# Both halves of every odd mixture chunk on GpSimd, VectorE casting the even chunks only

## What is computed

```python
# first mixture: 8 experts, 256 hidden units each, exact gelu
h = gelu(einsum('nd,edh->enh', xf, W1) + b1)        ; o = einsum('enh,ehd->end', h, W2) + b2
# second mixture: 8 experts, 512 hidden units each, tanh gelu
hid = gelu(einsum('bnd,edf->bnef', y, W1) + b1)     ; eo = einsum('bnef,efd->bned', hid, W2) + b2
```

## Time and profile before

| | |
|---|---|
| median of 3 runs | 4318.03 us (4313.71 to 4323.68) |
| span of the profiled execution | 4319.1 us |
| TensorE busy | 4066.8 us (94%) |
| VectorE busy | 3367.6 us (78%) |
| ScalarE busy | 2784.5 us (64%) |
| GpSimd busy | 2596.6 us (60%) |
| TensorE clock granted, mean | 0.983 of full speed |

### The profile page before, as it was taken

How to read it: one execution, slowest core, us unless ns; L and a number is a source line. 1 busy time by engine, 2 the same in 40 slices (tenths; PEclk the granted TensorE clock), 3 DMA queues, 4 the chain that set the end, 5 groups by cost and what they waited for, 6 DMA issues and landing times.

```text
span 4319.1 us, 104773 instructions
## 1 busy us (share of the span) xinstructions
PE 4066.8 (94%) x41344; PEld 3009.8 (70%) x41344; DVE 3367.6 (78%) x8878; ACT 2784.5 (64%) x4796; POOL 2596.6 (60%) x2494
## 2 busy tenths in 40 slices
PE   7678999999999999999999999999999999999998
PEld 3346777777777777777777777777777777777766
DVE  3357888888888888888888888878888887888876
ACT  3235766666676666667666666766666676666654
POOL 2034666666666666666666666666666666666656
PEclk9779999999999999999999999999999999999999
DMA  4200000011100001110000111000101100010000
GB/s 149 68 27 28 18 18 29 28 30 30 30 19 24 22 28 30 30 30 18 23 23 28 30 30 30 23 26 16 30 28 30 30 23 26 16 30 28 28 16 6
DMA packets 136939, 127.62 MB, mean 30 GB/s; under 512 B 28928, under 2 KB 135360, under 8 KB 136448
## 3 DMA queue, kind: packets, MB, share of 16 engines
q1 hardware_dynamic: 136448, 120.91, 9.6%
HBM read 71.05 MB, written 49.55 MB: 28 GB/s over the span
## 4 chain that ended last, share of the span: by engine, by line
PE 56%; DVE 24%; ACT 6%; POOL 5%; issue 4%; DMA 3%; SPq 2%; ACTq 0%; DVEq 0%; POOLq 0%
PE pf L1301 9%; PE pf L1303 8%; PE pf L1302 8%; PE pa L1561 8%; DVE h L1285 4%; PE pa L1447 3%; DVE hid_hi L1266 3%; PE pa L1543 3%; PE pa L1346 2%; PE pa L1433 2%; POOL inv_norm L650 2%; PE pa L1301 2%; ACT xn L726 2%; PE pa L1641 2%; PE pa L1303 2%
## 5 line engine op out<-in xcount | busy, mean ns | idle before, releaser
L660 POOL TENSOR_TENSOR hid_lo<-hid,hid_hi 128x504 f16<-128x504 f32 x1536 | 1835.5, 1212 | 775.8 <-DVE hid_hi L1266 775.8
L886 ACT ACTIVATE hid<-pf,vec 128x504 f32<-128x504 f32 x1536 | 1014.7, 680 | 505.5 <-PE pf L1303 356.9
L1301 PE MATMUL pf<-w_hi,hid_hi 128*126 128x128 f16 x6144 | 1133.7, 224 | 10.7 <-DVE h L1285 10.2
L1303 PE MATMUL pf<-w_hi,hid_lo 128*126 128x128 f16 x6144 | 1115.8, 221 | 0.0
L1302 PE MATMUL pf<-w_lo,hid_hi 128*126 128x128 f16 x6144 | 1115.4, 221 | 0.0
L1301 PEld LDWEIGHTS pf<-w_hi,hid_hi 128*126 128x126 f16 x6144 | 844.1, 137 | 153.5 <-issue 53.2
L1302 PEld LDWEIGHTS pf<-w_lo,hid_hi 128*126 128x126 f16 x6144 | 843.8, 137 | 28.5 <-issue 0.2
L1266 DVE CAST hid_hi<-hid 128x504 f16<-128x504 f32 x1536 | 845.4, 573 | 8.2 <-ACT hid L886 2.7
L1303 PEld LDWEIGHTS pf<-w_hi,hid_lo 128*126 128x126 f16 x6144 | 845.2, 138 | 0.0
L1285 DVE SCALAR_TENSOR_TENSOR h<-pf,gates,h 126x128 f32<-126x128 f32 x2048 | 574.1, 342 | 155.2 <-PE pf L1303 152.6
L616 POOL TENSOR_TENSOR pt<-pt,band 126x262 f32<-126x262 f32 x512 | 351.2, 707 | 527.6 <-ACT pt L773 527.4
(11 more groups left out here) (208 smaller groups left out, 7486.8 us busy)
## 6 DMA issues: line engine op xcount, KB each, us to landing
qk_spread<-terms SPq DMA_DIRECT2D x224, 126.0 KB, 2.5
qk_spread<-terms SPq DMA_DIRECT2D x192, 63.0 KB, 2.3
y_scratch<-hid SPq DMA_DIRECT2D x32, 252.0 KB, 2.1
y_in<-y_scratch SPq DMA_DIRECT2D x32, 252.0 KB, 3.2
terms<-qk_hi SPq DMA_DIRECT2D x32, 252.0 KB, 2.5
terms<-qk_lo SPq DMA_DIRECT2D x32, 252.0 KB, 2.6
qk_spread<-terms SPq DMA_DIRECT2D x32, 252.0 KB
terms<-ot_hi SPq DMA_DIRECT2D x32, 252.0 KB, 2.4
```

The source lines that it names most:

```text
L660: nc.gpsimd.tensor_tensor(hid_lo[:, c % 8], hid[:, c % HIDS], hid_hi[:, c % 8], ALU.subtract).then_inc(hid_lo_done[c % 2], 1)
L886: nc.scalar.activation(hid[:, c % HIDS], pf[:, c % 2, 0:TOK], func, bias=vec[:, bias:bias + 1]).then_inc(F["hid_ready"], 1)
L1301: nc.tensor.matmul(out, ah, bh, start=start, stop=False, skip_group_check=skip)
L1303: return nc.tensor.matmul(out, al, bh, start=False, stop=stop, skip_group_check=skip)
```

## The change

GpSimd now waits for ScalarE's gelu on odd chunks, makes the high half itself with a copy that casts, waits for its own copy to have been written, and subtracts as before. On even chunks it waits for VectorE's cast as before, under a semaphore that counts even chunks alone. VectorE skips odd chunks. The letters' orders, the buffers and all other work stay.

```diff
-POOL_EVEN = True
-        F = {name: sem(name) for name in "pre_ready hid_ready hid_hi_done hid_used gated".split()}
+        F = {name: sem(name) for name in "pre_ready hid_ready hid_hi_even hid_hi_odd hid_used gated".split()}
 # GpSimd
             def hidden(kind, p, c):
                 _, before = chunks_before(kind, p)
-                if c % 2 == 1 or POOL_EVEN:
-                    pool.wait_ge(F["hid_hi_done"], n(before + c + 1))
-                    nc.gpsimd.tensor_tensor(hid_lo[:, c % 8], hid[:, c % HIDS], hid_hi[:, c % 8],
-                                            ALU.subtract).then_inc(hid_lo_done[c % 2], 1)
+                done = (before + c) // 2 + 1
+                if c % 2 == 1:
+                    pool.wait_ge(F["hid_ready"], n(before + c + 1))
+                    nc.gpsimd.tensor_copy(hid_hi[:, c % 8], hid[:, c % HIDS]).then_inc(F["hid_hi_odd"], 1)
+                    pool.wait_ge(F["hid_hi_odd"], n(done))
+                else:
+                    pool.wait_ge(F["hid_hi_even"], n(done))
+                nc.gpsimd.tensor_tensor(hid_lo[:, c % 8], hid[:, c % HIDS], hid_hi[:, c % 8],
+                                        ALU.subtract).then_inc(hid_lo_done[c % 2], 1)
 # VectorE
             def hidden(kind, p, c):
                 _, before = chunks_before(kind, p)
-                dve.wait_ge(F["hid_ready"], n(before + c + 1))
-                nc.vector.tensor_copy(hid_hi[:, c % 8], hid[:, c % HIDS]).then_inc(F["hid_hi_done"], 1)
-                if c % 2 == 0 and not POOL_EVEN:
-                    ...
+                if c % 2 == 0:
+                    dve.wait_ge(F["hid_ready"], n(before + c + 1))
+                    nc.vector.tensor_copy(hid_hi[:, c % 8], hid[:, c % HIDS]).then_inc(F["hid_hi_even"], 1)
```

More of the change, by code:

```diff
@@ L1264, in hidden @@
                 _, before = chunks_before(kind, p)
-                dve.wait_ge(F["hid_ready"], n(before + c + 1))
-                nc.vector.tensor_copy(hid_hi[:, c % 8], hid[:, c % HIDS]).then_inc(F["hid_hi_done"], 1)
-                if c % 2 == 0 and not POOL_EVEN:
-                    dve.wait_ge(F["hid_hi_done"], n(before + c + 1))
-                    nc.vector.tensor_tensor(hid_lo[:, c % 8], hid[:, c % HIDS], hid_hi[:, c % 8],
-                                            ALU.subtract).then_inc(hid_lo_done[0], 1)
+                if c % 2 == 0:
+                    dve.wait_ge(F["hid_ready"], n(before + c + 1))
+                    nc.vector.tensor_copy(hid_hi[:, c % 8], hid[:, c % HIDS]).then_inc(F["hid_hi_even"], 1)
             def output(kind, p, j):
```

## The result

The changed kernel takes 4458.36 us (median of 4 runs, 4453.2 to 4467.1), the kernel before 4319.29 us in the same comparison. The ratio is 1.0331, with a 95% interval of 1.0314 to 1.0349: 3.3% slower, 139 us. I had forecast 4414 us, slower, between 4335 and 4500.

The account below looks back on a forecast made before the run. TensorE was taken as near its limit, busy 121.64 of 126.10 us a round. Terms 0.9 + 1.3 + 1.0 + 0.2 - 0.3 = 3.1 us, times 31 = 96 us, gave 4318 + 96 = 4414 us; range 4335 to 4500.

Parts of the forecast that it names:

- the likeliest stretch: Whole kernel: the summed forecast's most probable range, 4385 to 4450 us, chance 0.50.
- place A: After the inverse norm: GpSimd's low halves end later, delaying gelu, table load and TensorE by 1.0 us a round.
- place C: The band: two spots where slack of 0.53 and 0.58 us nearly covers a copy; together 0.2 us a round.
- The copy: GpSimd's cast of one odd chunk: 0.61 us, plus 0.06 waiting on its own semaphore; 16 us a round.
- R3: Rival: the copy is dear, 1.14 us giving 4578 us, 0.76 to 0.9 giving 4460 to 4505; chance 0.15.
- D: Second norm: three odd copies add 2.0 us, less 0.17, 0.3 and 0.2; `rstd` and TensorE 1.3 us later.
- B: First norm of the linear attention: three odd copies add 2.0 us, partly hidden; 0.9 us new TensorE wait a round.
- The step by step working: After the inverse norm: copy, L1215 and subtractions taking turns, ending at 2136.2 instead of 2135.10, 1.1 us later.
- makes up nothing later: TensorE, whole round: its order is fixed, so whatever makes it wait longer is paid in full.
- The gain: Freed VectorE time reaches TensorE only ahead of the linear attention's DMAs: 0.3 us a round won.
- The last sign of being wrong: TensorE's waits on VectorE turn out to have been more than its own rows tell; no size given.
- Elsewhere I cost the copies at nothing: Other 14 odd chunks: GpSimd's waits for casts hide the copies; without that cover, up to 9 us a round.

Follow-up runs that it names:

- experiment 9: Against the kernel before, GpSimd makes only the two odd high halves of place A (chunks 3 and 5, first mixture): 4335.98 us, ratio 1.0044.
- experiment 8: Against the kernel before, GpSimd makes only three odd high halves of place B (chunk 15, first mixture; 1 and 3, second): 4366.25 us, ratio 1.0091.
- experiment 7: Against the kernel before, GpSimd makes only the three odd high halves of place D (chunks 25, 27, 29, second mixture): 4373.11 us, ratio 1.0102.
- experiment 11: Against the kernel before, GpSimd makes only two high halves, chunk 31 of the second mixture and chunk 1 of the first: 4387.24 us, ratio 1.0159.
- experiment 1: Against the kernel before, VectorE skips the odd casts and GpSimd doesn't make them; odd high halves keep old values: 4285.70 us, ratio 0.9906.
- experiment 2: The kernel before with all VectorE casts, plus a GpSimd copy of every odd chunk to a spare tile: 4530.39 us, ratio 1.0474.
- experiment 5: The changed kernel with GpSimd's squares waiting behind VectorE's top-2 gates in rounds 1 to 30: 4411.01 us, ratio 1.0198 to the kernel before.
- experiment 3: Meant to put the squares behind the gates, but the test never held: the changed kernel run again, 4463.95 us, ratio 1.0320 to the kernel before.
- experiment 4: Against the kernel before, GpSimd makes only the 12 of 24 odd high halves a round outside places A to D: 4361.65 us, ratio 1.0082.

## Why the prediction came out right, and where its terms were off

The direction and the main mechanism held: TensorE, in its fixed order, pays for delays in GpSimd's bursts, and the loss goes by place, not by count. That the number fell into the range is in part luck. 4458 us lies above the likeliest stretch, 4385 to 4450, in the one that was given to a dearer copy, and the copy was not dear. By place, two, three, three and two copies (experiments 9, 8, 7, 11) make +0.44%, +0.91%, +1.02% and +1.59%, and ten others make -0.28%. These sum to 3.7% against the 3.3% of the change; they are not quite additive, since half a clock and place A stand in for each other. The four copies left, chunks 9, 13, 15 and 17 of the second mixture at place C, were in no experiment by themselves.

- The copy: 0.61 us taken, 0.60 measured. R3, the dear copy, falls.
- D: +1.3 taken. +1.06 in the changed kernel, +1.42 alone. Near, with the parts off: the three copies cost 1.88 (2.0 taken) and VectorE's relief gave 0.81 (0.5 taken).
- B: +0.9 taken, +1.35 measured. The step that read this place off GpSimd's order alone made it too small: VectorE's cast and its variance instruction, held up to 1.3 and 1.1 us, make the maxima late first.
- A: +1.0 taken, 0.55 measured. The step by step working had the first low half 1.7 us late (2133.2 against 2131.52), and TensorE's matmul there starts 1.42 late; but I let the shift pass on in full. TensorE's waits of 0.18 and 0.62 us behind it were there to absorb it, and did. The sentence that TensorE "makes up nothing later" was too strong.
- C: +0.2 taken, no jump of that size in the changed kernel's round.
- The gain: -0.3 taken, at the linear attention's DMAs. The trace of the round shows -0.29 at `xt_lo` and -0.16 at the maxima instead, besides the 0.81 inside D; experiment 1 bounds it all at -1.3. The last sign of being wrong, waits on VectorE that are more than its own rows tell, did show itself there. Still VectorE's 13.8 us a round were worth at most a tenth.
- "Elsewhere I cost the copies at nothing": this is the step that failed most. The copies of the two chunks ahead of the squares had slack themselves, but moved the squares from behind to ahead of the gates. The term it left out, 2.03 us a round and the clock behind it, is more than all that I was short of: 139 us measured less 96 forecast are 1.4 us a round. The other terms together were 0.6 us a round too dear, and hid the rest of it.

With the measured terms the sum is 1.35 + 1.06 + 0.55 + 2.03 - 0.29 - 0.16 = 4.5 us a round, and 31 times that 140 us, against 4.3 to 4.7 us a round in the trace; where the clock fell it stands in for A.

What remains open: how much of the 26 us by which the cost alone (experiment 2) exceeds change and gain together belongs to each of the differences named there. The rows put the shorter `xt_lo` down to the last copy ahead of the squares; the experiments show it for the pair of chunks only, not for each. And no run shows why only some of the long waits brought the clock down.

## What to carry to other kernels

Price moved work by the place where it lands: an engine at 60% of the span had no room at four places (A, B, D and ahead of the squares), and 10 of the 24 copies a round could be moved at a gain (12 with the squares out of the way). For an engine pair that holds each other up, list the short instructions on the critical path that run just ahead of a long one of the other engine; here a shift of 0.43 us between the two turned 0.19 us into 1.80. If one of the two has to wait, put the long instruction explicitly behind the short one: that took 1.3 points of the 3.3 off (experiment 5).

## What the hardware showed that I had not expected

A VectorE instruction on 32 numbers a partition with two SBUF inputs took 1.80 us beside GpSimd's squares, and one on four numbers 1.12 us: the hold does not follow the size of what is held, but what runs beside it. The Trainium skill's "SBUF — State Buffer", section "Who interferes with whom", tells this as an exclusive lock; by that rule the trace agrees, with 0.191 us in every round once the order is set (experiment 5).

After TensorE had stood 1.90 us, its granted clock fell to 1.2 GHz for 3.41 us in ten places of the steady part; there a round loses more than the wait itself, by 0.2 us on average in experiment 3 and 0.6 in experiments 4 and 11. With the wait at 0.3 us (experiment 5) it fell in none, though TensorE still waited 1.75 us for `xn` in every round.
